# Joining the context loads of the first two batches of a gated cross-attention and expert kernel

## What is computed

```python
x = x + jnp.tanh(g_xattn[0]) * _L0_xattn_ref(_layernorm(x, axis=-1), ctx_1024, ctx_1024)
x = x + jnp.tanh(g_ffn[0]) * _L0_ffn_ref(_layernorm(x, axis=-1), L0_ffn_gate_w, L0_ffn_gate_b, L0_ffn_w1, ...)

def _L0_xattn_ref(x, w1, w2):          # x: 8 x 112 x 256, w1 = w2 = context: 8 x 375 x 256
    h = jnp.einsum('eth,efh->etf', x, w1)
    g = jax.nn.gelu(h, approximate=True)
    return jnp.einsum('etf,efh->eth', g, w2)

def _L0_ffn_ref(x, gate_w, gate_b, w1, b1, w2, b2):
    top1 = jnp.argmax(xf @ gate_w.T + gate_b, axis=-1)
    for e in range(n_experts):         # 8 experts, hidden size 1024
        h = jax.nn.relu(xf @ w1[e].T + b1[e])
        y = h @ w2[e].T + b2[e]
        out = out + jnp.where((top1 == e)[:, None], y, 0)
```

## Time and profile before

| | |
|---|---|
| time, median of 3 runs | 111.12 us (110.9 to 111.33) |
| the profiled execution | 111.79 us, of which the span of the trace is 110.0 us |
| mean granted TensorE clock | 0.991 of full speed |
| busy | PE 100.7, PEld 92.7, DVE 53.5, ACT 28.6, POOL 39.9 us |
| moved by DMA | 28.36 MB, mean 258 GB/s |

### The profile page before, as it was taken

One profiled execution on the slowest core, in us unless ns is written; L12 is line 12 of the kernel. 1 busy time (PEld: TensorE's weight loads), 2 busy tenths in 40 slices (PEclk: granted clock), 3 DMA queues, 4 the chain that ended last, 5 costly groups with the idle time before them and its releaser, 6 DMA issues.

```text
span 110.0 us, 2150 instructions
## 1 busy us (share of the span) xinstructions
PE 100.7 (92%) x704; PEld 92.7 (84%) x705; DVE 53.5 (49%) x204; ACT 28.6 (26%) x91; POOL 39.9 (36%) x97
## 2 busy tenths in 40 slices
PE   5999899999999997799999999999999999999900
PEld 5998669999988895799989999899999998998600
DVE  0461578669689884796555332344133241333010
ACT  5616143212351440152302303223032140220000
POOL 3276386353664937700330557030030030300330
PEclk9999999999999999999999999999999999999996
DMA  3999999999995202599999999999992010010101
GB/s 80 316 331 246 404 419 422 404 427 426 413 414 202 86 0 65 128 352 359 368 416 402 419 420 365 415 426 426 432 419 114 7 44 0 0 40 6 46 19 35
DMA packets 6734, 28.36 MB, mean 258 GB/s; under 512 B 1149, under 2 KB 2511, under 8 KB 4672
## 3 DMA queue, kind: packets, MB, share of 16 engines
q1 hardware_dynamic: 4688, 25.09, 58.2%
q0 software_dynamic: 864, 2.12, 6.3%
q10 hardware_dynamic: 1168, 0.98, 2.8%
HBM read 26.33 MB, written 2.11 MB: 259 GB/s over the span
## 4 chain that ended last, share of the span: by engine, by line
PE 71%; DMA 11%; DVE 6%; issue 3%; POOL 2%; SPq 2%; ACTq 0%; ACT 0%; POOLq 0%; DVEq 0%
PE bank L978 29%; PE bank L987 26%; DMA x<-in_x_rest 8%; PE bank L928 6%; PE bank L910 5%; DMA region<-x_rows,from_row 3%; PE bank L960 2%; PE bank L919 2%; DVE x L582 1%; SPq L241 1%; PE bank L900 1%; POOL out_rows L386 1%; DVE stats L589 1%; SPq L231 1%; DVE region L791 1%
## 5 line engine op out<-in xcount | busy, mean ns | idle before, releaser
L978 PE MATMUL bank<-region,w 128*128 128x128 f32 x288 | 34.7, 277 | 0.3 <-ACT region L485 0.3
L978 PEld LDWEIGHTS bank<-region,w 128*128 128x128 f32 x288 | 33.8, 192 | 0.8 <-ACT region L485 0.4
L987 PE MATMUL bank<-w,region 128*128 128x256 f32 x144 | 32.6, 379 | 0.0
L987 PEld LDWEIGHTS bank<-w,region 128*128 128x128 f32 x144 | 26.7, 190 | 3.2
L520 ACT ACTIVATE region<-bank,smalls 128x128 f32<-128x128 f32 x40 | 12.5, 363 | 39.9 <-PE bank L978 38.5
L386 POOL DMA_INDIRECT out_rows<-region,to_row x9 | 8.9, 989 | 33.9 <-DVE region L813 32.4
L797 DVE TENSOR_SCALAR region<-bank,smalls 128x128 f32<-128x128 f32 x32 | 9.7, 346 | 13.8 <-PE bank L978 13.4
L381 POOL DMA_INDIRECT region<-x_rows,from_row x9 | 9.3, 1032 | 15.7 <-DMA region<-x_rows,from_row 12.2
L813 DVE SCALAR_TENSOR_TENSOR region<-bank,tg,region 128x256 f32<-128x256 f32 (+1 forms) x9 | 4.4, 484 | 19.0 <-PE bank L987 19.0
L910 PEld LDWEIGHTS bank<-xnT,region 128*125 128x125 f32 x96 | 11.4, 188 | 2.2 <-issue 1.6
L910 PE MATMUL bank<-xnT,region 128*125 128x120 f32 x96 | 12.0, 275 | 0.8 <-issue 0.7
(11 more groups left out here) (118 smaller groups left out, 85.7 us busy)
## 6 DMA issues: line engine op xcount, KB each, us to landing
w<-in_w1t SPq DMA_DIRECT2D x8, 1024.0 KB, 23.3
w<-in_w2t SPq DMA_DIRECT2D x8, 1024.0 KB, 26.5
region<-in_ctx SPq DMA_DIRECT2D x5, 771.0 KB, 13.2
region<-in_ctx SPq DMA_DIRECT2D x3, 396.0 KB, 9.1
region<-in_ctx SPq DMA_DIRECT2D x3, 375.0 KB, 4.2
x_rows<-x ACTq DMA_DIRECT2D x8, 113.8 KB, 6.4
b2b<-in_b SPq DMA_DIRECT2D x1, 896.0 KB
x<-in_x_rest SPq DMA_DIRECT2D x1, 586.2 KB, 8.3
```

What stands on the lines that cost most here:

```text
L978: mm = pe.matmul(hT_ps[k][:, part % 2 * P:(part % 2 + 1) * P], w1[:, e, n * H + part * P:n * H + (part + 1) * P], xgT[:, j % 2, n * P:(n + ...
L987: mm = pe.matmul(y[:, 0:D], hidT[:, q, part, :], w2[:, e, part * D:(part + 1) * D], start=(part == 0), stop=(part == KH - 1))
```

## The change

`HEAD` goes from 3 to 2. The contexts of batches 0 and 1 come from an HBM array of their own, `ctx_pair`, in which the two transposed parts stand first and the two row parts behind them; each of the two halves is one transfer (`pair_T`, 128 x 1500 floats, 750 KB; `pair`, 128 x 1584 floats, 792 KB) with one semaphore. The tile `region` is laid out to match, over the same bytes. The context of batch 2 is loaded whole, as those of 3 to 7 were. The tokens of batch 2 move into `x_rest`, which now holds six batches instead of five.

```diff
-HEAD = 3
+HEAD = 2
...
-        cxT, cx = cxs[:, :, 0:KD * CTX], cxs[:, :, KD * CTX:CW]
+        pair_T, pair = region[:, 0:HEAD * KD * CTX], region[:, HEAD * KD * CTX:HEAD * CW]
...
+        def context_T(b):
+            if b < HEAD:
+                return pair_T[:, b * KD * CTX:(b + 1) * KD * CTX]
+            return cxs[:, b, 0:KD * CTX]
...
-            load_x(0).then_inc(x_in[0], 16)
-            load_context_T(0)
-            load_x(1).then_inc(x_in[1], 16)
-            load_context_T(1)
-            load_x(2).then_inc(x_in[2], 16)
-            load_context_rows(0)
-            sp.dma_start(x2[0:S, HEAD:B, :], x_rest).then_inc(x_in[3], 16)
-            load_context_T(2)
-            load_context_rows(1)
-            load_context_rows(2)
-            for b in range(3, B):
-                load_context(b)
+            for b in range(HEAD):
+                load_x(b).then_inc(x_in[b], 16)
+            sp.dma_start(pair_T, ctx_pair[:, 0:HEAD * KD * CTX]).then_inc(pair_T_in, 16)
+            sp.dma_start(x2[0:S, HEAD:B, :], x_rest).then_inc(x_in[HEAD], 16)
+            sp.dma_start(pair, ctx_pair[:, HEAD * KD * CTX:HEAD * CW]).then_inc(pair_in, 16)
+            for b in range(HEAD, B):
+                sp.dma_start(cxs[:, b, :], ctx[b - HEAD]).then_inc(cx_in[b - HEAD], 16)
...
-                act.wait_ge(cx_in[b], 16)
+                act.wait_ge(pair_in if b < HEAD else cx_in[b - HEAD], 16)
...
-                pe.wait_ge(cxT_in[b] if b < 3 else cx_in[b], 16)
+                pe.wait_ge(pair_T_in if b < HEAD else cx_in[b - HEAD], 16)
```

More of the change, by code:

```diff
@@ L54, with gated_cross_attention_moe @@
 NOWHERE = 65536.0
-def gated_cross_attention_moe(nc, x, x_rest, ctx, small, w1t, w2t, b2, out):
+def gated_cross_attention_moe(nc, x, x_rest, ctx_pair, ctx, small, w1t, w2t, b2, out):
     x2_dram = nc.dram_tensor("x2_rows", (TOKENS, ROW), F32, kind="Internal").ap()
@@ L174, in ranks, with context_rows @@
             return {3: banks[6], 6: banks[1], B - 1: banks[6]}.get(b, rk_ps)
-        x_in = [sem("x_in0"), sem("x_in1"), sem("x_in2"), sem("x_in3")]
+        def context_T(b):
+            if b < HEAD:
+                return pair_T[:, b * KD * CTX:(b + 1) * KD * CTX]
+            return cxs[:, b, 0:KD * CTX]
+        def context_rows(b):
+            if b < HEAD:
+                return pair[:, b * CC * DL:(b + 1) * CC * DL]
+            return cxs[:, b, KD * CTX:CW]
+        x_in = [sem("x_in0"), sem("x_in1"), sem("x_in2")]
         small_in, b2_in = sem("small_in"), [sem("b2_in0"), sem("b2_in1")]
-        cxT_in = [sem("cxT_in0"), sem("cxT_in1"), sem("cxT_in2")]
-        cx_in = [sem(f"cx_in{b}") for b in range(B)]
+        pair_T_in, pair_in = sem("pair_T_in"), sem("pair_in")
+        cx_in = [sem(f"cx_in{b}") for b in range(HEAD, B)]
         w1_in = [sem(f"w1_in{e}") for e in range(E)]
@@ L226, in _ @@
         def _(sp):
[L227 to L234, removed]
             def load_expert(e):
@@ L461, in gate_share @@
                 scored = sc_ps[b % 2][0:CR, 0:CC * SL].rearrange("p (c n) -> p c n", c=CC)
-                act.wait_ge(cx_in[b], 16)
-                act.activation(cx[0:CR, b, :].rearrange("p (c n) -> p c n", c=CC)[:, :, D:DL], scored[:, :, S:SL],
+                act.wait_ge(pair_in if b < HEAD else cx_in[b - HEAD], 16)
+                act.activation(context_rows(b)[0:CR, :].rearrange("p (c n) -> p c n", c=CC)[:, :, D:DL], scored[:, :, S:SL],
                                ACT.Copy).then_inc(cg_ok, 1)
@@ L910, in scores @@
                         mm = pe.matmul(sc_ps[b % 2][0:CR, c * SL:(c + 1) * SL],
-                                       cxT[:, b, k * CTX + c * CR:k * CTX + (c + 1) * CR],
+                                       context_T(b)[:, k * CTX + c * CR:k * CTX + (c + 1) * CR],
                                        xnT[:, b % 2, k * SL:(k + 1) * SL], start=(k == 0), stop=(k == KD - 1))
@@ L928, in attend @@
                     mm = pe.matmul(at_ps[b % 2][0:S, 0:DL], gel[0:CR, b % 2, c * S:(c + 1) * S],
-                                   cx[0:CR, b, c * DL:(c + 1) * DL], start=(c == 0), stop=(c == CC - 1))
+                                   context_rows(b)[0:CR, c * DL:(c + 1) * DL], start=(c == 0), stop=(c == CC - 1))
                 mm.then_inc(at_done, 1)
@@ L1144 @@
     from concourse.bass_utils import run_bass_kernel_spmd
+    ctx = np.asarray(ctx_1024)
+    ctx_T = ctx.transpose(0, 2, 1).reshape(B, KD, P, CTX).transpose(0, 2, 1, 3).reshape(B, P, KD * CTX)
+    ctx_rows = np.pad(ctx.reshape(B, CC, CR, D).transpose(0, 2, 1, 3),
+                      ((0, 0), (0, P - CR), (0, 0), (0, DL - D))).reshape(B, P, CC * DL)
     arrays = {
@@ L1150 @@
                                                  ((0, 0), (0, 0), (X0, E)))),
-        "ctx": np.ascontiguousarray(np.concatenate([
-            np.asarray(ctx_1024).transpose(0, 2, 1).reshape(B, KD, P, CTX).transpose(0, 2, 1, 3).reshape(B, P, KD * CTX),
-            np.pad(np.asarray(ctx_1024).reshape(B, CC, CR, D).transpose(0, 2, 1, 3),
-                   ((0, 0), (0, P - CR), (0, 0), (0, DL - D))).reshape(B, P, CC * DL)], axis=2)),
+        "ctx_pair": np.ascontiguousarray(np.concatenate([*ctx_T[0:HEAD], *ctx_rows[0:HEAD]], axis=1)),
+        "ctx": np.ascontiguousarray(np.concatenate([ctx_T[HEAD:B], ctx_rows[HEAD:B]], axis=2)),
         "small": np.ascontiguousarray(np.concatenate([
```

## The result

The changed kernel takes 115.34 us (median of 4 executions, 114.15 to 116.85) against 111.22 us for the kernel before (110.90 to 111.81). The ratio is 1.033, with a 95% interval of 1.023 to 1.043: slower by 3.6 us, with 2.5 and 4.8 us as the ends of that interval; in the medians of all executions it is 4.1 us. A loss of 1.0 us was forecast.

What follows compares the result with a forecast made beforehand. TensorE, busy 92% of the span, bounds the kernel; its run of batches starts 1.0 us later. So 111.8 + 1.0 = 112.8 us profiled, 0.67 above the median: 112.1 us, range 111.6 to 112.8, 8 in 10 110.7 to 113.3.

Steps and rivals of the forecast that it cites:

- `pair_T` ends at 974 KB: 6.4 us: Start of the queue: the joined transposed part lands at 6.4 us, so `scores(0)`, before at 6.45, loses about nothing.
- the old curve of bytes against time: Load queue: landing times by KB queued in the kernel before, such as 974 KB at 6.4 us, assumed for the changed queue.
- The later landings: Loads after `pair_T`: on the curve, `x_rest` in at 10.5 us, joined rows at 12.75, batch 2's context at 14.65.
- The term called decisive: Ahead of `scores(2)`: waiting for batch 2's whole context moves it from 12.70 to 14.4 us, TensorE's run 1.0 us later.
- this tie: Ahead of `scores(2)`: `attend(0)` ends at 14.45 us, just as the wait for batch 2's context ends at 14.4.
- Rival 3: TensorE's clock falls in the stall ahead of `attend(0)`: 1 to 3 us on top, 113.1 to 115 us; chance 0.08.
- The gain of 0.3 us from joining: Start of the queue: joined transfers flow better, taken as 0.3 us between bounds of no gain and 1.15 us.
- rival 2: Slow stretch from 7 to 11 us goes too: 2.55 us less loss, `scores(4)` 1.2 us early, 109.9 us; chance 0.12.
- rivals 1 and 2: The first: better flow at the start just pays for the wait, 111.3 us, chance 0.22; the second: 109.9 us, chance 0.12.
- The slow stretch: Transfers from 7 to 11 us at 267 GB/s, worth 1.4 us: unexplained, left in place, neither gain nor loss counted.
- `norm_x(2)` behind `x_rest` and `attend(0)` behind the joined rows: New waits: batch 2's tokens come with `x_rest` at 10.5 us; joined rows at 12.75 move `attend(0)` from 10.72 to 13.1.
- no wait for a transfer after `scores(2)`: TensorE's later batches: contexts already in, `scores(3)` 3.4 us behind `scores(2)` and `scores(4)` near 21.0 us.

Runs made afterwards that it cites:

- a_warm: Changed kernel with nine instead of one warm-up matmul on TensorE ahead of `scores(0)`; 113.36 us, ratio 1.019 to the kernel before.
- b_ctx2_warm: Kernel before with only batch 2's context loaded whole, plus eight warm-up matmuls ahead of `scores(2)`; median 112.35 us, ratio 1.012.
- a_joined_second: Changed kernel with the joined transposed part second in the queue, ahead of batch 1's tokens; 111.26 us in one execution.
- b_rest128: Kernel before with `x_rest` loaded over 128 instead of 112 partitions, 16 rows of zeros added; 110.27 us, ratio 0.992.
- a_order: Changed kernel with the joined transposed part cut into its two halves, in the same place of the queue; 111.99, 112.13, 114.08 and 116.22 us.
- a_t_split: Changed kernel with the transposed parts of batches 0 and 1 loaded apart, each behind its tokens; 112.16, 115.52, 114.01 and 115.38 us.
- a_rest128: Changed kernel with `x_rest` loaded over 128 instead of 112 partitions; ten executions from 110.91 to 116.2 us.
- b_ctx2_whole: Kernel before with only batch 2's context loaded whole, behind batch 1's rows; 113.53, 113.81, 114.07 and 111.84 us.

## Why the prediction was wrong

The direction was right; the size was not, 4.1 us in the medians instead of 1.0. By its steps:

- **The step that failed is the first: "`pair_T` ends at 974 KB: 6.4 us ... so this costs about nothing".** It rested on the assumption that the changed queue lands along the old curve of bytes against time. The joined part landed at 8.36 us, with two short transfers ahead of the first long one; put second in the queue, it lands at 6.0. `scores(0)` went from 6.45 to 8.49, and TensorE stood still for 1.86 us where the prediction had no gap. That gap set off the lower clock.
- **The later landings failed with the same assumption.** `x_rest` was in at about 11.5 us instead of 10.5, the joined rows at 13.1 instead of 12.75, the context of batch 2 at 15.1 instead of 14.35. With the clock held up (a_warm) the run of batches starts 1.9 us late in the trace (`scores(4)` at 21.97 on the chain, against 20.03), where 1.0 was forecast, and the kernel loses 1.9%, or 2.1 us.
- **The term called decisive, `scores(2)`'s wait for the whole context of batch 2**, is real and somewhat small where it stands alone: forecast 1.0 us, measured 1.3 (b_ctx2_warm). But it is not what delayed the changed kernel. There `scores(2)` started 2 us after that context was in; in a_warm it started at 15.35 behind `attend(0)`, on a chain from `x_rest`, with the context in at 15.2. The prediction had this tie too (14.45 and 14.4) and named only one side of it. How the 2.1 us divide between the two paths is not shown; to bring only one of them forward would have won 0.2 us at most.
- **Rival 3, the clock, came true; I gave it 0.08.** It cost 1.6 to 2.0 us. The price of 1 to 3 us was right and the chance far too small. I had compared a gap of 2.4 us that the prediction itself made, with one gap of 1.19 us in the trace, and took the one example for safety. I also placed the gap ahead of `attend(0)` only; the one that came first lay ahead of `scores(0)`, where TensorE had done little but warm-up before. Four of four executions of the changed kernel show the lower clock in their means.
- **The gain of 0.3 us from joining** was not there in the changed kernel: 255 and 236 GB/s in the two early stretches against 316 and 267. Whether joining gains something in another order stays open. In a_joined_second the rate from 2 to 7 us is 324 GB/s, about that of before, but from 7 to 11 us it is 355, and the context of batch 2 is in early enough for rival 2's condition (by 12.8 us). In the kernel as it was changed, rivals 1 and 2 both failed.
- **The slow stretch** ("I leave it where it is") moved with `x_rest`, as the remark on rival 2 suspected, and began earlier. I had noted that it starts when `x_rest` comes to the front and drew nothing from it, though a gain lay behind it: 0.8% (b_rest128).
- **Held:** `norm_x(2)` behind `x_rest` and `attend(0)` behind the joined rows as new waits; no wait for a transfer after `scores(2)`; the shift handed on unchanged from `scores(4)` to the end. **Missed as well:** TensorE's gap of about 2 us ahead of `attend(0)`, which in the changed kernel the slowed matmuls filled.

Of the 4.1 us, then, 2.0 are the clock and 2.1 the transfers that came late or are waited for longer, of which 1.0 was forecast.

## What to carry to other kernels

When transfers are joined, ask for each consumer when the *whole* of the new transfer is in, and do not trust an old curve of bytes against time at the start of the queue: here the order of the first three transfers alone moved a landing from 8.36 to 6.0 us. Each new wait of TensorE has two prices, the wait and the clock that may fall behind it; fill the gap with matmuls that compute nothing and see which of the two you pay. Where two waits end together, name both, since to mend one wins next to nothing. And a transfer that runs far below the rate of its neighbours with all DMA engines busy deserves a look at how many partitions it fills.

## What the hardware showed unexpectedly

- A transfer over 112 of 128 partitions with rows of 5360 bytes held the whole queue at 267 GB/s; over 128 partitions, with more bytes, it ran at 388. Two halves of 64 partitions with rows of 6168 bytes, one behind the other, brought 251, and whole transfers of such rows in the same stretch 420. The reason is not shown.
- The granted clock fell to 0.50 after TensorE had stood for 1.86 us ahead of `scores(0)`. It fell only at about 9.5 us, 1.0 us after the work had begun again, and stayed down through unbroken matmuls until about 16.3 us. Kernels whose traces show a gap of 1.28 us (a_order), 1.39 (a_t_split), 1.64 (a_rest128) or 2.00 (b_ctx2_whole) in the first 15 us had the lower clock in some executions and not in others. With a gap of 1.19 us in its trace (a_warm), or with the gap filled (b_ctx2_warm), none of 14 executions had a mean clock under 0.984.
- The same 750 KB transfer landed 4.8 us after its issue as the second in the queue, and 6.7 us as the third. Of one and the same queue of loads, the same transfer was in at 14.0 us in one trace and 15.0 in another (b_ctx2_whole, b_ctx2_warm).
